# Second expert layer turned round, and expert results summed in memory by accumulating scatters

## What is computed

```
h = layernorm(x) * (1 + cb) + sb
logits = silu(h @ rw1 + rb1) @ rw2 + rb2
k_logits, k_index = top_k(logits, 2);  k_prob = softmax(k_logits)
for e in range(8):
    we = sum(where(k_index == e, k_prob, 0))
    out += we * (silu(h @ w1[e] + b1[e]) @ w2[e] + b2[e])     # 128 -> 512 -> 128
x = x + gb * out
```

## Time and profile before

| | |
|---|---|
| median of 3 runs | 386.02 us |
| span of the profiled execution (first to last instruction) | 388.5 us |
| PE busy | 309.1 us (80%) |
| PE weight loads | 242.7 us (62%) |
| DVE busy | 194.7 us (50%) |
| ACT busy | 133.3 us (34%) |
| POOL busy | 174.2 us (45%) |
| chain that ended last, by engine | PE 73%, DVE 11%, ACT 5%, DMA 4% |

### The profile page before, as it was taken

How to read it: one execution, slowest core, us unless ns; L and a number is a source line. 1 busy time by engine, 2 the same in 40 slices (tenths; PEclk the granted TensorE clock), 3 DMA queues, 4 the chain that set the end, 5 groups by cost and what they waited for, 6 DMA issues and landing times.

```text
span 388.5 us, 6416 instructions
## 1 busy us (share of the span) xinstructions
PE 309.1 (80%) x1736; PEld 242.7 (62%) x1737; DVE 194.7 (50%) x791; ACT 133.3 (34%) x267; POOL 174.2 (45%) x188
## 2 busy tenths in 40 slices
PE   0295839999999999710799999999999999999200
PEld 0252415669667865710588888888888888888200
DVE  3879899773677722240243333333343333432187
ACT  1049989322322242000243333433344333443000
POOL 1806282087576855762044444444444444444300
PEclk9999877866868786555599999999999999999755
DMA  7950000011010111114322212222211212200398
GB/s 227 324 172 14 0 2 2 0 37 49 29 54 29 50 41 50 41 62 117 83 54 59 58 54 61 61 67 56 56 47 45 69 41 61 60 29 13 86 321 241
DMA packets 41635, 28.39 MB, mean 73 GB/s; under 512 B 5463, under 2 KB 38273, under 8 KB 41616
## 3 DMA queue, kind: packets, MB, share of 16 engines
q1 hardware_dynamic: 32498, 17.56, 16.4%
q0 software_dynamic: 4544, 8.47, 6.7%
q10 hardware_dynamic: 4574, 2.13, 1.9%
HBM read 16.39 MB, written 12.67 MB: 75 GB/s over the span
## 4 chain that ended last, share of the span: by engine, by line
PE 73%; DVE 11%; ACT 5%; DMA 4%; SPq 3%; issue 3%; POOL 1%; POOLq 0%; DVEq 0%
PE bank L897 19%; PE bank L885 18%; PE bank L833 11%; PE bank L845 10%; PE bank L877 4%; PE bank L899 3%; PE bank L856 3%; PE bank L771 2%; DMA xs<-in_L_attn_x_dram 1%; DMA av<-expert_out 1%; DVE st L521 1%; PE bank L858 1%; SPq L315 1%; ACT hT L436 1%; SPq L307 1%
## 5 line engine op out<-in xcount | busy, mean ns | idle before, releaser
L412 POOL DMA_INDIRECT expert_out<-tx,dest_t x78 | 76.8, 985 | 109.3 <-DVE tx L738 102.8
L494 ACT ACTIVATE tx<-bank,w_t 128x256 f32<-128x256 f32 x156 | 65.0, 471 | 129.9 <-PE bank L885 129.2
L897 PE MATMUL bank<-w_s,tx 128*128 x624 | 86.4, 281 | 0.0
L401 POOL DMA_INDIRECT sorted_rows<-rows,sloti x64 | 64.1, 1002 | 39.5 <-DVE sloti L647 22.4
L897 PEld LDWEIGHTS bank<-w_s,tx 128*128 128x128 f32 x624 | 78.6, 191 | 4.6
L885 PE MATMUL bank<-h2T,w_t 128*128 128x256 f32 x312 | 75.9, 387 | 0.0
L738 DVE TENSOR_SCALAR tx<-bank,prob_t 128x128 f32<-128x128 f32 x78 | 27.3, 350 | 80.5 <-PE bank L899 80.5
L885 PEld LDWEIGHTS bank<-h2T,w_t 128*128 128x128 f32 x312 | 57.6, 195 | 6.8 <-DVE w_t L730 0.3
L833 PE MATMUL bank<-h2T,rw_s 128*128 128x512 f32 x64 | 45.7, 881 | 0.8 <-ACT h2T L467 0.8
L724 DVE COPY h2T<-bank 128x256 f32<-128x256 f32 x39 | 16.6, 424 | 44.2 <-PE bank L877 34.0
L877 PE MATMUL bank<-ident,tx 128*128 128x128 f32 x78 | 17.7, 310 | 19.9 <-DMA tx<-sorted_rows 19.9
(11 more groups left out here) (158 smaller groups left out, 343.6 us busy)
## 6 DMA issues: line engine op xcount, KB each, us to landing
tx<-sorted_rows SPq DMA_DIRECT2D x39, 130.0 KB, 2.2
w_s<-in_L_ffn_w_dram SPq DMA_DIRECT2D x16, 256.0 KB, 5.9
xs<-in_L_attn_x_dram SPq DMA_DIRECT2D x8, 256.0 KB, 4.6
av<-expert_out SPq DMA_DIRECT2D x8, 256.0 KB, 4.9
qv<-expert_out SPq DMA_DIRECT2D x8, 256.0 KB, 5.7
expert_out<-tx,dest_t POOLq DMA_INDIRECT x78, 2.3
sorted_rows<-padr SPq DMA_DIRECT2D x9, 130.0 KB, 2.6
sorted_rows<-rows,sloti POOLq DMA_INDIRECT x64, 2.3
```

What stands on the lines that cost most here:

```text
L401: p.indirect_dma_start(sorted_rows[:, :], bass.IndirectOffsetOnAxis(ap=sloti[:, k, t:t + 1], axis=0), rows[:, t, k, :], None).then_inc(s_d ...
L412: p.indirect_dma_start(expert_out[:, :], bass.IndirectOffsetOnAxis(ap=dest_t[:, s % U, n, :], axis=0), yo[:, s % 2, n, :], None, bounds_ch ...
L494: ins = nc.scalar.activation(hsT[:, u % 2, h, :], bank[2 + 2 * (u % 2) + q][:, (h % 2) * SL:(h % 2 + 1) * SL], ACT.Silu, bias=w1_t[:, u % ...
L897: t.matmul(o, hsT[:, u % 2, h, n * P:(n + 1) * P], w2_s[:, bass.ds(e * (HC * D) + h * D, D)], start=(h == 0), stop=False)
```

## The change

The second layer is computed like the first. w2 of the expert is copied by DVE to a fixed place `w2_t` together with b2 as one extra column, the four blocks of w2 stay in the array in turn, and the 256 columns of `hsT` stream past each. The result now has features on partitions, so ACT can add b2 as a bias while it moves the result out of PSUM (`bias_out`), and two transposes on PE (`turn_y`) bring rows back on partitions. DVE then scales both halves in one instruction. PE's order becomes `turn_x(s+1)`, `layer1(s)`, `turn_y(s-2)`, `layer2(s-1)`.

The scatters add into one DRAM array `acc` with one row per token (and 256 for padding). SP fills it with zeros first. Two scatters of different steps may now meet the same row, so POOL waits, before the two scatters of a step, until those of the step before have landed. At the end there is one load per group and no addition of two parts.

```
-        expert_out = nc.dram_tensor("expert_out", [TOPK * TOK, D], F32)
+        acc = nc.dram_tensor("acc", [TOK + SL, D], F32)
...
+            sp.wait_ge(s_const, 7)
+            for g in range(NG):
+                sp.dma_start(acc[g * G:(g + 1) * G, :].rearrange("(n p) d -> p n d", p=P),
+                             zeros[:, :, :]).then_inc(s_acc, 16)
...
-                for k in range(TOPK):
-                    sp.dma_start(y01[g][:, k, :, :],
-                                 expert_out[k * TOK + g * G:k * TOK + (g + 1) * G, :]
-                                 .rearrange("(n p) d -> p n d", p=P)).then_inc(s_y01[g], 16)
+                sp.dma_start(mix[g], acc[g * G:(g + 1) * G, :]
+                             .rearrange("(n p) d -> p n d", p=P)).then_inc(s_mix[g], 16)
...
+                p.memset(zeros[:, :, :], 0.0)
...
+            pool.wait_ge(s_acc, 16 * (NG + 1))
             for s in range(TILES):
+                pool.wait_ge(s_yo, s + 1)
+                if s:
+                    pool.wait_ge(s_sc[(s - 1) % U], 16 * HALVES * rounds(s - 1, (s - 1) % U))
                 for n in range(HALVES):
-                    pool.wait_ge(s_yo, HALVES * s + n + 1)
                     p.indirect_dma_start(
-                        expert_out[:, :], bass.IndirectOffsetOnAxis(ap=dest_t[:, s % U, n, :], axis=0),
-                        yo[:, s % 2, n, :], None, bounds_check=last_row, oob_is_err=False).then_inc(s_sc[s % U], 16)
+                        acc[:, :], bass.IndirectOffsetOnAxis(ap=pd_i[:, s % U, n, 1:2], axis=0),
+                        yo[:, s % 2, n, :], None, compute_op=ALU.add).then_inc(s_sc[s % U], 16)
...
+            def bias_out(s, u):
+                act.wait_ge(s_l2, s + 1)
+                if not (static(s) and s < 2):
+                    act.wait_ge(s_yturn, s - 1)
+                nc.scalar.activation(yT[:, u % 2, :], bank[6][:, 0:SL], ACT.Identity,
+                                     bias=w2_t[:, u, HC * D:W2E]).then_inc(s_yT_e, 1)
...
             def prepare(s, u, e):
+                v.tensor_copy(w1_t[:, u % 2, :], w1_s[:, bass.ds(e * WE, WE)])
+                if not (static(s) and s < U):
+                    dve.wait_ge(s_yT_e, s - U + 1)
+                v.tensor_copy(w2_t[:, u, :], w2_s[:, bass.ds(e * W2E, W2E)]).then_inc(s_w12t, 1)
+                dve.wait_ge(s_txp, s + 1)
                 v.tensor_copy(xT[:, u % 2, :], bank[u % 2][:, 0:SL]).then_inc(s_xT, 1)
...
             def scale_y(s, u):
+                dve.wait_ge(s_yturn, s + 1)
+                if not (static(s) and s < 2):
+                    dve.wait_ge(s_sc[(u - 2) % U], 16 * HALVES * rounds(s - 2, (u - 2) % U))
+                v.tensor_tensor(yo[:, u % 2, :, :], bank[7][:, 0:SL].rearrange("p (n d) -> p n d", n=HALVES),
+                                pd_t[:, u, :, 0:1].to_broadcast([P, HALVES, D]), ALU.mult).then_inc(s_yo, 1)
...
-                f0 = y01[g][:, 0, :, :]
-                link(v.tensor_tensor(f0, f0, y01[g][:, 1, :, :], ALU.add))
+                f0 = mix[g]
...
+            def layer2(s, u):
                 pe.wait_ge(s_hs, 2 * (s + 1))
+                if not (static(s) and s < 1):
+                    pe.wait_ge(s_yT_e, s)
+                for h in range(HC):
+                    ins = t.matmul(bank[6][:, 0:SL], w2_t[:, u, h * D:(h + 1) * D], hsT[:, u % 2, h, :],
+                                   start=(h == 0), stop=(h == HC - 1))
+                ins.then_inc(s_l2, 1)
+
+            def turn_y(s, u):
+                pe.wait_ge(s_yT_e, s + 1)
+                if not (static(s) and s < 1):
+                    pe.wait_ge(s_yo, s)
                 for n in range(HALVES):
+                    ins = t.transpose(bank[7][:, n * P:(n + 1) * P], yT[:, u % 2, n * P:(n + 1) * P], ident[:, :])
+                ins.then_inc(s_yturn, 1)
```

More of the change, by code:

```diff
@@ L42, in adaln_block @@
     WE = HID + HC
+    W2E = HC * D + 1
     U = 4
@@ L51, in adaln_block, with cols_ @@
     with ExitStack() as ctx:
+        def cols_(g):
+            return slice(g * G, (g + 1) * G)
         def sb(name, shape, dt=F32):
@@ L70, in adaln_block @@
         w1_s = sb("w1_s", [P, NE * WE])
-        w2_s = sb("w2_s", [P, NE * HC * D])
+        w2_s = sb("w2_s", [P, NE * W2E])
         wmod_s = sb("wmod_s", [P, 6 * D])
-        NSM = B + 1 + HC + NE * HC
+        NSM = B + 1 + HC + NE * HC + NE
         small = sb("small", [NSM, P])
@@ L79, in adaln_block @@
         rb1_s = smallT[:, B + 1:B + 1 + HC]
-        b1_c = smallT[:, B + 1 + HC:NSM].rearrange("p (e h) -> p e h", h=HC)
+        b1_c = smallT[:, B + 1 + HC:NSM - NE].rearrange("p (e h) -> p e h", h=HC)
+        b2_c = smallT[:, NSM - NE:NSM].unsqueeze(2)
         wx_c = sb("wx_c", [P, HB])
@@ L96, in adaln_block @@
         half_neg = sb("half_neg", [P, GT])
[L97 to L100, removed]
+        zeros = sb("zeros", [P, GT, D])
         st1 = sb("st1", [P, NT, 6])
@@ L162, in adaln_block @@
         yo = in_tx(2 * HALVES * D).rearrange("p (r n d) -> p r n d", r=2, n=HALVES)
+        yT = sb("yT", [P, 2, SL])
         xT = h2T[:, :, 0:SL]
-        prob_t = sb("prob_t", [P, U, HALVES, 1])
-        dest_t = sb("dest_t", [P, U, HALVES, 1], I32)
+        pd_t = sb("pd_t", [P, U, HALVES, 2])
         w1_t = sb("w1_t", [P, 2, WE])
-        y01 = [z[:, i * TOPK * G:(i + 1) * TOPK * G].rearrange("p (k n d) -> p k n d", k=TOPK, d=D)
-               for z in (av, qv) for i in range(NG // 2)]
+        w2_t = sb("w2_t", [P, U, W2E])
+        mix = [av[:, cols_(g)].rearrange("p (n d) -> p n d", d=D) for g in range(NG)]
         bank = [ps(f"bank{i}", [P, 512]) for i in range(8)]
@@ L197, in adaln_block @@
         s_xr = sems(*(f"s_xr{i}" for i in range(U)))
-        s_txp, s_xT, s_w1t, s_l1, s_hs, s_l2, s_yo, s_fin = sems(
-            "s_txp", "s_xT", "s_w1t", "s_l1", "s_hs", "s_l2", "s_yo", "s_fin")
-        s_taken, s_out = sems("s_taken", "s_out")
+        s_txp, s_xT, s_w12t, s_l1, s_hs, s_l2, s_yT_e, s_yturn, s_yo, s_fin = sems(
+            "s_txp", "s_xT", "s_w12t", "s_l1", "s_hs", "s_l2", "s_yT_e", "s_yturn", "s_yo", "s_fin")
+        s_taken, s_out, s_acc = sems("s_taken", "s_out", "s_acc")
         s_sc = sems(*(f"s_sc{i}" for i in range(U)))
-        s_y01 = sems(*(f"s_y01_{g}" for g in range(NG)))
+        s_mix = sems(*(f"s_mix{g}" for g in range(NG)))
         rows_i = rows[:, :, :, :].bitcast(I32)
         padr_i = padr[:, :, :].bitcast(I32)
-        xr_i = xr.bitcast(I32)
+        pd_i = pd_t[:, :, :, :].bitcast(I32)
         block = ctx.enter_context(nc.Block())
@@ L298, in _ @@
                 sp.dma_start(w1_s[:, e * WE:e * WE + HID], w1[e]).then_inc(s_w1, 16)
-                sp.dma_start(w2_s[:, e * HC * D:(e + 1) * HC * D].rearrange("p (c d) -> p c d", c=HC),
+                sp.dma_start(w2_s[:, e * W2E:e * W2E + HC * D].rearrange("p (c d) -> p c d", c=HC),
                              w2[e].rearrange("(c p) d -> p c d", p=P)).then_inc(s_w2, 16)
-            sp.wait_ge(s_b2p, 1)
-            for k in range(3):
-                sp.dma_start(b2_s[k:k + 1, :], b2_p[:, k, :]).then_inc(s_b2s, 16)
+            sp.wait_ge(s_const, 7)
+            for g in range(NG):
+                sp.dma_start(acc[g * G:(g + 1) * G, :].rearrange("(n p) d -> p n d", p=P),
+                             zeros[:, :, :]).then_inc(s_acc, 16)
+            sp.dma_start(acc[TOK:TOK + SL, :].rearrange("(n p) d -> p n d", p=P),
+                         zeros[:, 0:HALVES, :]).then_inc(s_acc, 16)
             def padding(row):
@@ L421, in _ @@
             act.dma_start(small[B + 1:B + 1 + HC, :], rb1.rearrange("(h p) -> h p", p=P)).then_inc(s_small, 16)
-            act.dma_start(small[B + 1 + HC:NSM, :], b1.rearrange("e (h p) -> (e h) p", p=P)).then_inc(s_small, 16)
+            act.dma_start(small[B + 1 + HC:NSM - NE, :], b1.rearrange("e (h p) -> (e h) p", p=P)).then_inc(s_small, 16)
+            act.dma_start(small[NSM - NE:NSM, :], b2).then_inc(s_small, 16)
             act.dma_start(wx_c[:, :], w_in.rearrange("h d e -> (h d) e")).then_inc(s_wc, 16)
@@ L497, in hidden, with step @@
                     ins.then_inc(s_hs, 1)
-            expert_steps(act, hidden, TILES)
+            def bias_out(s, u):
[4 more added lines that the diff above has]
+                                     bias=w2_t[:, u, HC * D:W2E]).then_inc(s_yT_e, 1)
+            def step(s, u):
+                if not static(s) or s >= 2:
+                    bias_out(s - 2, (u - 2) % U)
+                if not static(s) or s < TILES:
+                    hidden(s, u)
+            expert_steps(act, step, TILES + 2)
             for g in range(NG):
                 act.wait_ge(s_fin, g + 1)
-                act.dma_start(out_t[:, tiles(g), :], y01[g][:, 0, :, :]).then_inc(s_out, 16)
+                act.dma_start(out_t[:, tiles(g), :], mix[g]).then_inc(s_out, 16)
             act.wait_ge(s_out, 16 * NG)
@@ L727, in prepare @@
                     dve.wait_ge(s_sc[u], 16 * HALVES * (rounds(s, u) - 1))
```

(37 more changed lines are left out.)

28 lines of the change are left out of this document (8 added, 20 removed).

## The result

The changed kernel takes 450.25 us (median of 4 runs, 449.41 to 451.10) against 386.22 for the kernel before in the same series: ratio 1.162, 95% interval 1.156 to 1.168. I had forecast 396 us with a range of 368 to 427. The sign was right, the size was not: the loop of scatters is far longer than I made it.

A forecast was written before the change was run, and what follows sets the result against it. POOL's scatter loop was to replace PE as the bound: first scatter at 199.5 us, 39 loops of 4.67 less the last wake-up to 381.3, plus 16.9 gives 398.2, less 2.5 some 396 us; range 368 to 427.

The forecast's parts named there:

- The sign: Whole kernel: the change was forecast to make it slower, 9.7 us over the span of 388.5; chance of slower 0.70.
- PE's part: PE in the expert steps: two layers of 1.73 us and two transpose pairs of 0.28 make a step of 4.02 us.
- POOL's loop: POOL's scatters, step to step: second scatter, its landing and POOL's wake-up make 4.67 us, 0.65 more than PE's step.
- 1.29 to the second scatter: POOL within a step: the second scatter starts 1.29 us after the first, read from plain scatters.
- The landing: Accumulating scatter, start to landing: 3.1 us, 0.8 more than a plain one, for reading the old row first.
- The wake-up of POOL: POOL between a landing and its next scatter: 0.28 us, as read after DVE's instruction.
- Read and write in sequence: Rival on the accumulating scatter: a whole read behind a whole write, landing 4.5 us, loop 6.07, 450 us; chance 0.12.
- The accumulate is cheap: Rival on the scatter: landing at most 2.8 us, PE's 4.02 or a loop up to 4.4 sets the step, 367 us; chance 0.27.
- PE's clock: Rival on PE: idle time lowers its clock, a step at 1.2 GHz takes 8.2 us, a tenth of them gives 410; chance 0.04.
- POOL held off by DVE: Rival on POOL: DVE's large copies cost it up to 2 x 0.42 us a step, loop 5.5, 428 us; chance 0.04.
- First scatter: Start of the expert stretch: with the deeper pipeline the first scatter goes at 199.5 us, where it was 196.48.
- after the last landing: End of the kernel: one load per group and no addition take 16.9 us in place of 23.8, 6.9 less.

The follow-up runs named there:

- run 6: Against the kernel before: turned second layer, plain scatters into separate rows, no wait on POOL, DVE's scaling ahead of its small copy; 376.17 us, ratio 0.959.
- run 3: Against the kernel before: only the turned second layer, with plain scatters into separate rows, no wait on POOL, two loads per group at the end; 395.31 us, ratio 0.998.
- run 4: Against the kernel before: turned second layer, scatters adding into separate zeroed rows, no wait on POOL; 453.32 and 460.52 us, no ratio formed.
- run 1: The kernel after with DVE's scaling put ahead of its copy of probability and row number; 454.26 us, ratio 1.147 to the kernel before.
- run 2: The kernel after with scatters that overwrite instead of adding, all waits kept; 395.97 us, ratio 1.003 to the kernel before.
- run 8: The kernel after with DVE's scaling ahead of its small copy and POOL's two waits in the other order; 440.13 us, ratio 1.122 to the kernel before.
- run 7: Against the kernel before: turned second layer, scatters adding into separate zeroed rows, no wait on POOL, DVE's scaling ahead of its small copy; 388.15 us, ratio 0.990.

## Why the prediction was right or wrong

- **Sign and mechanism.** A loop of scatter, landing and next scatter replaced PE as the bound, as forecast, with POOL's scatters in pairs and PE idle, as I said the profile would show. Half right: the loop closes through DVE's small copy, and not where I had closed it, in POOL's own wait.
- **PE's part.** 4.02 us forecast, 3.90 measured (run 6); a pair of transposes is 0.22, not 0.28. Right within 0.12.
- **POOL's loop, the step that failed.** "The loop becomes 1.29 + 3.1 + 0.28 = 4.67 us." Measured 5.92, and 6.05 on average. The terms:
  - 1.29 to the second scatter was taken from plain scatters; it is 1.85, since POOL works 1.55 us on an accumulating one. Too low by 0.56. I had named "if POOL needs much longer than 0.98" as a way to be wrong, but gave it no place in the range.
  - The landing, 3.1 forecast, 3.27 measured: 0.17. The part that I thought most uncertain was nearly right, and 0.57 of the 1.0 us it grew by is POOL's own work again, as it counts from the scatter's start.
  - "The wake-up of POOL is 0.28" left out DVE: copy, scaling and POOL's start are 0.80. Too low by 0.52. I had counted DVE's slack ("2.2 us of 4") and its wait for scatters of step s-2, but not the wait of the small copy for step s-3, which stands ahead of the scaling in the queue. Runs 3 and 4 show this ring without POOL's wait, run 6 shows it gone. Without DVE in it the term would still have been 0.73 (run 1), for POOL's own start after a landing with the waits in this order: the 0.28 was read where only DVE's rows were waited for.
  - Together 1.25 a step, 49 us over 39; with the average of 6.05 it is 54, as much as the miss from 396 to 450.
- **The rivals.** "Read and write in sequence" gave 450 us, the measured time, for the wrong reason: its landing of 4.5 us was 3.27. A hit on the time proves nothing of the mechanism. "The accumulate is cheap" was wrong: the landing is 3.27, not at most 2.8, and without the addition the new kernel is level with the kernel before (run 2). And its price was wrong too: 367 us for a cheap landing overlooked that DVE's ring holds even plain scatters at 4.4 (middle pairs of runs 2 and 3). PE's clock held at 0.96 over the expert stretch.
- **POOL held off by DVE.** Where DVE's copies of the next step start while a scatter is at work, the scatter can take 1.70 instead of 1.55 (run 8, at 309.45; the first of the copies starts at 310.19), and a copy up to 0.77 instead of 0.42 (run 7, at 307.62, within the scatter that starts at 307.11). The rival's 0.84 a step was too much; POOL loses up to 0.2 on a scatter. The Trainium skill, "SBUF — State Buffer", "Who interferes with whom", gives the ports that GpSimd shares with a DVE instruction in two-port mode to whoever issues first, and has the other wait for that whole instruction. Here the scatter starts first in both rows and both engines lose time, neither by the whole of the other's work: the rows show that the two get in each other's way, but not a wait for the whole instruction.
- **The edges.** First scatter at 197.6, forecast 199.5; after the last landing 16.6, forecast 16.9. Right.

The Trainium skill's figures for an access to HBM ("DMA: Bandwidth & Descriptors", "Latency and other measured facts") had given a landing of 2.5 or 4.3 us as an estimate; 3.27 lies between, and neither end would have been of use.

## What to carry to other kernels

When a pipeline gets one stage deeper, recount every ring of buffers and every wait in front of the moved instruction in its engine's queue: a copy of four numbers per partition that waits for a free buffer closed a loop that cost the whole gain (ratio 0.998), and behind the scaling it cost nothing that the chain shows (0.959). Two loops of about the same length hide each other, so undoing one shows nothing; write both down from the chain of waits, and take away both. For a scatter that waits for the one before, price POOL's time twice, once up to the second scatter and once inside the landing, with the accumulating form's own duration.

## What the runs showed that I had not expected

- An accumulating scatter of 128 rows of 512 bytes holds POOL for 1.55 us against 0.98, and makes 144 packets against 32. From the end of POOL's record to the landing it is 1.72 us against 1.29: all that comes after POOL's work takes only 0.4 more.
- The order in which POOL's two waits are written is worth 0.46 us each time: 0.27 or 0.73 from the last condition to the scatter.
- DVE goes on 0.02 us after the same landing, and in run 1 POOL's own waiting instruction does too, so a landing is noticed at once; the rest lies between that instruction and POOL's start of the scatter.
